# First pass of the attention scores in 24 chunks of 384 columns, handed out by a table

## The reference

```python
x = x + attention(layernorm(x))      # twice normalised, with gamma and beta inside
x = x + experts(layernorm(x))        # router, best 2 of 8, gated by their probabilities
# attention, per head:
content   = (q + u_bias) @ k.T
pos_score = rel_shift((q + v_bias) @ p.T)
attn      = softmax((content + pos_score) / sqrt(128))
ctx       = attn @ v                 # then ctx @ Wo + bo
```

## Time and profile before

| | us |
|---|---|
| three runs | 1701.21, 1703.7, 1705.15 (median 1703.7) |
| the profiled execution | 1698.55 |
| its span, first to last instruction | 1696.8 |
| PE busy in the span | 1551.2 (91%) |
| DVE busy | 1402.8 (83%) |
| ACT busy | 1111.8 (66%) |
| POOL busy | 1105.3 (65%) |
| granted TensorE clock, mean | 0.948 |

### The profile page before, as it was taken

How to read it: one execution, slowest core, us unless ns; L and a number is a source line. 1 busy time by engine, 2 the same in 40 slices (tenths; PEclk the granted TensorE clock), 3 DMA queues, 4 the chain that set the end, 5 groups by cost and what they waited for, 6 DMA issues and landing times. The chain is left out here.

```text
span 1696.8 us, 50747 instructions
## 1 busy us (share of the span) xinstructions
PE 1551.2 (91%) x12534; PEld 1207.3 (71%) x12535; DVE 1402.8 (83%) x5272; ACT 1111.8 (66%) x2303; POOL 1105.3 (65%) x2090
## 2 busy tenths in 40 slices
PE   2599999999999999999999999999952699999997
PEld 1367677777677767777767776777741699999997
DVE  3389889989989988998998998799864588888886
ACT  2127776777777777777777777677730577777775
POOL 3337767776776776777677677567673276666666
PEclk8569999999999999999999999899975799999999
DMA  5624634643653463464355346246453243433433
GB/s 162 192 55 137 184 99 114 182 127 103 170 149 97 137 186 101 112 181 128 103 169 149 97 137 184 71 125 172 127 162 126 43 57 55 57 52 55 57 51 49
DMA packets 131859, 199.97 MB, mean 118 GB/s; under 512 B 18392, under 2 KB 93032, under 8 KB 131648
## 3 DMA queue, kind: packets, MB, share of 16 engines
q1 hardware_dynamic: 105792, 177.20, 36.9%
q0 software_dynamic: 25856, 20.27, 7.9%
HBM read 108.24 MB, written 75.33 MB: 108 GB/s over the span
## 5 line engine op out<-in xcount | busy, mean ns | idle before, releaser
L1063 DVE CUSTOM_DVE_ANT_0 junk<-pA,lmask 128x512 bf16<-128x512 f32 x1056 | 687.1, 683 | 67.6 <-PE pA L651 49.1
L965 ACT ACTIVATE prob<-pB 128x512 f32<-128x512 f32 x384 | 229.8, 599 | 200.9 <-PE pB L670 115.1
L1547 POOL DMA_INDIRECT out<-yb,dst x144 | 231.2, 1605 | 134.7 <-ACT yb L1621 82.7
L672 PE MATMUL pB<-QL,K 97*128 97x512 f32 (+3 forms) x768 | 285.2, 371 | 1.4 <-ACT upper_diag L965 1.2
L649 PE MATMUL pA<-K,QL 96*128 96x512 f32 (+3 forms) x792 | 284.0, 360 | 0.8 <-DVE acc L1069 0.4
L670 PE MATMUL pB<-QU,K 97*128 97x512 f32 (+3 forms) x640 | 266.7, 417 | 0.2
L967 ACT ACTIVATE prob<-pB 128x512 f32<-128x512 f32 x384 | 227.9, 593 | 12.4 <-PE pB L672 4.1
L651 PE MATMUL pA<-K,QU 96*128 96x512 f32 (+3 forms) x660 | 232.8, 354 | 1.6 <-DVE acc L1063 0.3
L688 PE MATMUL pC<-prob,vext 128*17 128x256 f32 x3088 | 217.3, 384 | 0.1
L556 POOL TENSOR_TENSOR prob<-prob,upper_diag 128x128 f32<-128x128 f32 x384 | 179.9, 469 | 31.9
L670 PEld LDWEIGHTS pB<-QU,K 97*128 97x128 f32 x640 | 121.6, 190 | 99.3 <-issue 61.7
(11 more groups left out here) (305 smaller groups left out, 3658.5 us busy)
## 6 DMA issues: line engine op xcount, KB each, us to landing
QL<-split_operands SPq DMA_DIRECT2D x67, 256.0 KB
QU<-split_operands SPq DMA_DIRECT2D x67, 256.0 KB
K<-split_operands SPq DMA_DIRECT2D x67, 256.0 KB
xg<-routed_rows SPq DMA_DIRECT2D x76, 132.0 KB
split_operands<-c_h SPq DMA_DIRECT2D x18, 512.0 KB
split_operands<-c_l SPq DMA_DIRECT2D x18, 512.0 KB
QL<-split_operands SPq DMA_DIRECT2D x67, 128.0 KB
QU<-split_operands SPq DMA_DIRECT2D x67, 128.0 KB
```

What stands on the lines that cost most here:

```text
L672: mm = pe.matmul(pB[:, q0 + up:q0 + HALF], K[0:r, s, k], QL[0:r, s, q0 + up:q0 + HALF], start=True, stop=True)
L965: act.activation(p[:, 0:HALF], pB[:, 0:HALF], ACT.Exp, scale=SCALE).then_inc(p_exp, 1)
L1063: v.tensor_tensor_reduce(out, src[:, :], lmask[:, at:at + HALF], 1.0, -3.0e38, ALU.add, ALU.max, acc[:, s, qb, n % 2:n % 2 + 1]).then_inc( ...
L1547: po.indirect_dma_start(dram["out"], bass.IndirectOffsetOnAxis(dst[k][:, a:a + 1], 0), yb[k][:, a, :], None, compute_op=ALU.add).then_inc( ...
```

## The change

The first pass of a head is cut into 24 chunks of 384 columns. For each of the 8 query blocks the row of scores is laid out as 1024 + 128 = 1152 columns: the lower form up to and with the diagonal block, then the upper form from the diagonal block on (so the diagonal block stands twice, once in each form). Three chunks of 384 make such a row. One mask `smask` (bf16) serves all: zeros, the lower diagonal's mask at block 7, the upper diagonal's at block 8, and the single column beyond at block 9. The diagonal pieces, `umask` and `ORDER` are gone; the three `pA` tiles stay 512 columns wide and 384 of them are used; `acc` takes three maxima per block (columns 0 to 2) in place of two and the diagonal's.

The table `SHARE[h][u]` says how many chunks unit u of head h takes (0 to 5, 24 per head; before, 2 pieces in each of 9 units). PE in a unit: second pass half 0, the first chunk, second pass half 1, chunks two and three, the contexts, and then what is left of the unit's chunks, ahead of the small pieces. DVE: the first chunk, the evacuation, all other chunks, its other work. The setup has one memset less on POOL.

```diff
+CHUNK = 3 * P
+SPANS = (S + P) // CHUNK
+S1U = NB * SPANS
-        lmask, umask = sb("lmask", [P, 15 * P], BF16), sb("umask", [P, P])
+        smask = sb("smask", [P, 16 * P], BF16)
-        ORDER = (0, 1, 2, 3, 4, 5, 6, 7, 16, 8, 9, 10, 17, 11, 12, 13, 14, 15)
+        SHARE = ((5, 1, 3, 3, 3, 4, 1, 3, 1), (4, 1, 1, 3, 3, 5, 2, 4, 1), (3, 2, 3, 1, 3, 4, 3, 1, 4), (1, 3, 1, 2, 4, 3, 3, 4, 3),
+                 (4, 3, 2, 1, 3, 4, 1, 2, 4), (3, 2, 0, 3, 5, 3, 2, 2, 4), (4, 3, 3, 3, 3, 4, 2, 1, 1), (5, 2, 2, 2, 4, 2, 1, 2, 4))
+        def share(h, u):
+            return range(sum(SHARE[h][:u]), sum(SHARE[h][:u + 1]))
         def piece(n):
+            qb, c = divmod(n, SPANS)
+            return qb, c, min(max(P * (qb + 1) - CHUNK * c, 0), CHUNK)
...
             # PE, first_pass
+                qb, c, low = piece(n)
+                q, k0 = slice(P * qb, P * qb + P), CHUNK * c
+                if low > 0:
+                    mm = pe.matmul(dst[:, 0:low], QL[0:KROWS, s, q], K[0:KROWS, s, k0:k0 + low], start=True, stop=True)
+                if low < CHUNK:
+                    mm = pe.matmul(dst[:, low:CHUNK], QU[0:KROWS, s, q], K[0:KROWS, s, k0 + low - P:k0 + CHUNK - P], start=True, stop=True)
                 mm.then_inc(s1_ready, 1)
...
             # PE, the loop
+                        chunks = share(h, u)
                         second_pass(b, h, u, 0)
-                        first_pass(b, h + AHEAD, 2 * u)
+                        for n in chunks[:1]:
+                            first_pass(b, h + AHEAD, n)
                         second_pass(b, h, u, 1)
-                        first_pass(b, h + AHEAD, 2 * u + 1)
+                        for n in chunks[1:S1_BUFS]:
+                            first_pass(b, h + AHEAD, n)
                         if u in PAIRS_AT:
                             back, kb = PAIRS_AT[u]
                             context(b, h + back, kb)
                             context(b, h + back, kb + 1)
+                        for n in chunks[S1_BUFS:]:
+                            first_pass(b, h + AHEAD, n)
...
             # DVE, first_pass
+                qb, c, _ = piece(n)
+                at = 7 * P - P * qb + CHUNK * c
+                v.tensor_tensor_reduce(out, src[:, 0:CHUNK], smask[:, at:at + CHUNK], 1.0, -3.0e38, ALU.add, ALU.max,
+                                       acc[:, s, qb, c:c + 1]).then_inc(s1_read, 1)
```

More of the change, by code:

```diff
@@ L28 @@
 HPB = S // HALF
-S1U = NB * HPB + HPB
+CHUNK = 3 * P
+SPANS = (S + P) // CHUNK
+S1U = NB * SPANS
 S2U = NB + 1
@@ L121, in attention_phase @@
         mrow = [sb(f"mrow{i}", [NB, P], F32R) for i in range(2)]
-        junk = sb("junk", [P, S1_BUFS, HALF], BF16)
+        junk = sb("junk", [P, S1_BUFS, CHUNK], BF16)
         ctxT = t3
@@ L234, in stored_to @@
             return dram["operands"][bass.ds(nb % 2, 1), op, :, 2 * low + row, :, :].rearrange("o h d s -> (o h) d s")
-        DVE_SET, DVE_BIAS, POOL_SET = 13, 11, 15
+        DVE_SET, DVE_BIAS, POOL_SET = 13, 11, 14
         D_W, D_CST = 16 * 8, 16 * 5
         EVEN, MOVED_N = P - 16, 48
-        ORDER = (0, 1, 2, 3, 4, 5, 6, 7, 16, 8, 9, 10, 17, 11, 12, 13, 14, 15)
+        SHARE = ((5, 1, 3, 3, 3, 4, 1, 3, 1), (4, 1, 1, 3, 3, 5, 2, 4, 1), (3, 2, 3, 1, 3, 4, 3, 1, 4), (1, 3, 1, 2, 4, 3, 3, 4, 3),
+                 (4, 3, 2, 1, 3, 4, 1, 2, 4), (3, 2, 0, 3, 5, 3, 2, 2, 4), (4, 3, 3, 3, 3, 4, 2, 1, 1), (5, 2, 2, 2, 4, 2, 1, 2, 4))
+        def share(h, u):
+            return range(sum(SHARE[h][:u]), sum(SHARE[h][:u + 1]))
         def piece(n):
-            qb, k0 = n // HPB, (n % HPB) * HALF
-            return qb, k0, min(max(P * (qb + 1) - k0, 0), HALF)
+            qb, c = divmod(n, SPANS)
+            return qb, c, min(max(P * (qb + 1) - CHUNK * c, 0), CHUNK)
         @block.sync
@@ L397, in _ @@
             po.memset(ident[:, :], 0.0).then_inc(set_pool, 1)
-            po.memset(lmask[:, :], 0.0).then_inc(set_pool, 1)
-            po.memset(umask[:, :], 0.0).then_inc(set_pool, 1)
+            po.memset(smask[:, :], 0.0).then_inc(set_pool, 1)
             po.memset(cmask[:, :, :], 0.0).then_inc(set_pool, 1)
@@ L404, in _ @@
             po.memset(mhalf[:, :], -0.5).then_inc(set_pool, 1)
-            po.wait_ge(set_pool, 9)
+            po.wait_ge(set_pool, 8)
             po.affine_select(out=ident[:, :], in_=ident[:, :], compare_op=ALU.not_equal, fill=1.0, base=0,
                              pattern=[[-1, P]], channel_multiplier=1).then_inc(set_pool, 1)
-            po.affine_select(out=lmask[:, 7 * P:8 * P], in_=lmask[:, 7 * P:8 * P], compare_op=ALU.is_ge, fill=FAR, base=0,
+            po.affine_select(out=smask[:, 7 * P:8 * P], in_=smask[:, 7 * P:8 * P], compare_op=ALU.is_ge, fill=FAR, base=0,
                              pattern=[[-1, P]], channel_multiplier=1).then_inc(set_pool, 1)
-            po.affine_select(out=umask[:, :], in_=umask[:, :], compare_op=ALU.is_ge, fill=FAR, base=-2,
+            po.affine_select(out=smask[:, 8 * P:9 * P], in_=smask[:, 8 * P:9 * P], compare_op=ALU.is_ge, fill=FAR, base=-2,
                              pattern=[[1, P]], channel_multiplier=-1).then_inc(set_pool, 1)
@@ L416, in _ @@
                              pattern=[[0, H], [P, NB]], channel_multiplier=1).then_inc(set_pool, 1)
-            po.affine_select(out=lmask[:, 8 * P:8 * P + 1], in_=lmask[:, 8 * P:8 * P + 1], compare_op=ALU.not_equal, fill=FAR, base=1 - P,
+            po.affine_select(out=smask[:, 9 * P:9 * P + 1], in_=smask[:, 9 * P:9 * P + 1], compare_op=ALU.not_equal, fill=FAR, base=1 - P,
                              pattern=[[0, 1]], channel_multiplier=1).then_inc(set_pool, 1)
@@ L1300, in _ @@
                                 small_piece(b, name)
-                        first_pass(b, h + AHEAD, 2 * u + 1)
+                        for n in chunks[1:]:
+                            first_pass(b, h + AHEAD, n)
                         if h == 0 and u in NORMALIZE_AT:
```

## The result

The changed kernel takes 1783.96 us (median; 1782.33 to 1786.45) against 1702.45 for the kernel before: 1.048 times as long, 95% interval 1.0461 to 1.0500. I had forecast 1660, and a range that ended at 1712.

The account below looks back on a forecast made before the run. It took DVE, 91% busy in the loop, as the scarce engine, often waiting on a late PE. 1698.55 - 44 (PE's 20 included) = 1654.6, carried by 5.2 to the timed median: 1660 us; range 1625 to 1712.

Parts of the forecast that it names:

- DVE's work: DVE's first pass: 0.477 us per 384-column instruction, 11.4 us per head before and after; loop busy time 1025 to 1040 us.
- The expert phase and the stages ahead of the loop: Expert phase runs none of the changed lines: unchanged; ahead of the loop, waits on diagonal pieces go, 1 us at most.
- PE's 20 us: PE's first pass in the loop: six fewer 128-column matmuls, 0.3 us less per head, 20 us, part of the 44.
- The order: New order of first-pass work in the loop: half of DVE's 88.4 us of waits on PE go, 44 us.
- The second rival: Units with 4 or 5 chunks: PE stands for tiles, 88 us, half lost, 44, cancelling the gain: 1704 us, chance 0.08.
- The third rival: Context units: three 384-column tiles hold too little DVE work, 69 us less 41 of diagonal waits: 1732 us, chance 0.16.
- My bound of 8 us: DVE's first pass: 0.02 us more for each of six more waits and registers, 0.1 us per head, 8 in all.

Follow-up runs that it names:

- even table: Changed kernel with every head's SHARE row 3, 2, 3, 3, 3, 3, 2, 3, 2; DVE's loop at slot 0 of a 256-instruction fetch block: 1703.04 us, 1.0035.
- b_head0: Kernel before, with DVE's loop code starting at slot 0 of a 256-instruction fetch block: 1711.59 us, 1.0075.
- a_bunch: Changed kernel, DVE's loop at slot 0, even table but two chunks moved into unit 0 from units 3 and 7: 1749.34 us, 1.0280.
- a_head0: Changed kernel with its own table, DVE's loop code starting at slot 0 of a 256-instruction fetch block: 1743.02 us, 1.0267 of the kernel before.
- b_padded_head0: Kernel before with 96 already met waits added in DVE's loop body, the loop starting at slot 0: 1712.97 us, 1.0055.
- after: The changed kernel as it stands, own table and own loop place, against the kernel before: 1783.96 us, 1.0481.
- a_slot128: Changed kernel with its own table, DVE's loop starting at slot 128 of a 256-instruction fetch block: 1737.54 us, 1.0222 of the kernel before.
- b_shift12: Kernel before, with DVE's loop moved 12 instruction slots on by already met waits ahead of it: 1704.36 us, 1.0028.
- b_padded: Kernel before with 12 met waits ahead of DVE's loop and 96 in it, giving the changed kernel's loop start and length: 1753.25 us, 1.0297.
- b_split: Kernel before, with the second first-pass piece of context units moved between the contexts of the two key blocks: 1774.77 us, 1.0439.

## Why the prediction was wrong

*DVE's work: right.* From 265.29 to 265.76 a 384-column instruction takes 0.47 us, and the median of the 957 that follow another without a gap is 0.478; I had 0.477. DVE's busy time in the loop is 1040.3 us, just over the 1025 to 1040 given.

*The expert phase and the stages ahead of the loop: as forecast,* since the whole loss lies in the loop; what comes behind it takes 446 us in place of 449.

*PE's 20 us: not shown.* No run has the shorter matmuls alone. The even table at slot 0 is 6 us over the kernel before and 7 under b_head0, and its batch at a clock of 1.00 takes 141.8 us against 141.5, so nothing of it is left in the time; whether the thinner stock took it or it never came through, no run tells.

*The order: the step that failed.* It stood in the sum as a gain of 44 us ("I take it that half of DVE's waits on PE go"). The table alone cost 39 to 45 us. I read its agreement with DVE's other work as evidence that DVE would be fed, and compared loads per unit only. What I had in hand spoke against it: the floor of 1.23 us means that a unit with 0 to 2 chunks can't pay back all that one with 5 costs (0.26 us came back for a chunk taken out, 0.42 were paid for one put in), and with three tiles PE can't run ahead of a bunch. DVE's waits on PE rose from 88 to 125 us, and at the even table, where the bunches are gone, they are back at the level before, 67.1 + 17.0 = 84 us:

```profile
DVE junk L1065 <- PE pA L654: 67.1, 117, 1.5
...
DVE junk L1065 <- PE pA L652: 17.0, 56, 0.4
```

So the waits weren't those of a badly shared first pass.

*The second rival named the mechanism and its price was close.* "PE stood for all of them" gave 88 us, half 44; the measured cost is 39 to 45. The half was a guess, and its coming out is partly luck: in a_bunch 128 chunks beyond the third, 61 us by the same count, cost 42, two thirds. The error was to set it off against a gain that didn't exist. As a loss alone it gives 1704 + 44 = 1748 us; a_head0, where the table acts without the pauses at the return, takes 1743.

*The third rival got the sign, but not by its cause.* Its 69 us for a thinner stock aren't there: the even table has the same three tiles of 384 and lands at 1.0035. A smaller cost of the stock, up to 26 us, isn't ruled out.

*What was missing: DVE's code, 31 to 44 us.* I counted six more waits and registers per head at 0.02 us each, a price that no row gave, as time in the queue; in that sense they cost nothing that shows (b_padded_head0's batch of 141.5 us). They are also 96 more instructions in a loop that was already long, and 12 ahead of it, and both are visible in the diff. My bound of 8 us for them was four to five times too small.

The measured steps from the kernel before: +0.0035 (384-column chunks, even table, slot 0), +0.0232 (the table), +0.0214 (the place of the code), which is 6 + 39 + 36 = 81 us on 1702.5. The pause at slot 0's entry, some 4 us, is in the first of them and so missing from the last.

## What to carry to other kernels

When three engines meet in every unit of work through a few tiles, compare a plan by the sum over units of the slowest engine's time with each unit's floor, not by how even one engine's load looks: what is piled on a unit was paid nearly in full here, what was taken out of one came back by half or less. Count the instructions that a change adds to a long loop's body, waits and register sums too, and after it look for idle time with no releaser at the loop's return; if there is some, move the loop's start before judging anything else in the change, and look at the loop's entry as well, where a new start can put a pause of its own. A pause costs more than its length when PE's clock is lower behind it.

## What the runs showed of the hardware

- DVE paused 4.3 to 6.0 us at each return of a 982-instruction loop body at one start of the code, and not at slots 0 and 128 (after, a_head0, a_slot128); with 886 instructions at the same start it didn't (b_shift12), and with 96 waits added to those it did (b_padded). In each of the 21 pauses a packet of the instruction queue starts 1.9 to 2.3 us before the end.
- At slot 0 the entry into the loop takes 3.8 to 4.6 us from the branch to the next instruction (eight traces), at slot 128 0.56 (two).
- In the 20 us behind such a pause the mean granted clock was 0.66 in b_padded, and 1.00 where there was no pause; b_padded's batches took 149.2 to 150.6 us between returns against 141.5, 7.7 to 9.1 more for a pause of 4.3 to 4.9.
- One ordinary matmul of 512 columns between the contexts of two key blocks cost PE 0.3 us per pair, beyond its own 0.24 (b_split). That it is the change between the two kinds of matmul is my reading; no run isolates it.
- One of three tiles less cost 2.7% with two pieces of 512 columns per unit and 15.7% with two or three of 384.
